# Expert stage of a three-block layer: 23 tiles of 256 sorted tokens of one expert in place of 40 of 128

## What is computed

```
x = x + cross_attention(norm(x), ctx)      # 16 heads, 257 context rows per sequence, 96 wide
x = x + time_mixing(norm(x))               # decayed running sums over the 32 positions
x = x + ffn(norm(x))
# ffn: expert = argmax(x @ Wr.T + br) of 8 experts; per token only that expert counts
h = relu(x @ W1[e].T + b1[e])              # 128 -> 512
y = h @ W2[e].T + b2[e]                    # 512 -> 128
```

## Time and profile before

| | |
|---|---|
| three runs | 1028.87, 1029.09 (median), 1031.62 us |
| span of the profiled execution, first to last instruction | 1027.0 us |
| busy: PE, DVE, POOL, ACT | 870.6, 831.1, 774.3, 684.0 us |
| scatter of the sorted rows, last landing | at 907.9 us |
| first product of the expert stage | at 913.2 us |
| start of the last indirect store | at 1019.8 us |

### The profile page before, as it was taken

One profiled execution on the slowest core, in us unless ns is written; L12 is line 12 of the kernel. 1 busy time (PEld: TensorE's weight loads), 2 busy tenths in 40 slices (PEclk: granted clock), 3 DMA queues, 4 the chain that ended last, 5 costly groups with the idle time before them and its releaser, 6 DMA issues.

```text
span 1027.0 us, 29818 instructions
## 1 busy us (share of the span) xinstructions
PE 870.6 (85%) x8554; PEld 720.6 (70%) x8554; DVE 831.1 (81%) x2343; ACT 684.0 (67%) x2029; POOL 774.3 (75%) x1237
## 2 busy tenths in 40 slices
PE   7989998999999999999999999999998461049895
PEld 7777786878787887878787887887776261036664
DVE  5899888989999989899999999998988657025563
ACT  3777776778777778778777777777775113037774
POOL 5788888898989898888889898989886503735554
PEclk9999999999999999999999999999999655559998
DMA  9111111111111111111111211111100840111120
GB/s 233 33 33 33 32 33 33 33 33 36 49 42 32 31 31 31 31 31 31 31 31 32 59 33 31 31 31 31 31 2 2 129 162 14 52 43 53 47 54 17
DMA packets 56836, 45.11 MB, mean 44 GB/s; under 512 B 8367, under 2 KB 54578, under 8 KB 56769
## 3 DMA queue, kind: packets, MB, share of 16 engines
q1 hardware_dynamic: 54464, 40.01, 15.9%
q0 software_dynamic: 2304, 4.25, 1.3%
HBM read 37.25 MB, written 7.52 MB: 44 GB/s over the span
## 4 chain that ended last, share of the span: by engine, by line
PE 36%; POOL 31%; issue 13%; DVE 12%; ACT 4%; DMA 1%; POOLq 1%; DVEq 1%; ACTq 0%; SPq 0%
POOL Pn L925 10%; PE bank L396 6%; PE bank L373 6%; PE bank L420 4%; POOL cT L916 4%; PE bank L1369 3%; PE bank L413 3%; PE bank L385 3%; POOL sorted_rows L1232 3%; POOL chi L906 2%; PE bank L1384 2%; DVE cs L839 2%; DVE nmax L783 2%; POOL clo L910 2%; DVE Tl L777 1%
## 5 line engine op out<-in xcount | busy, mean ns | idle before, releaser
L925 POOL TENSOR_TENSOR Pn<-Pe,rsum 128x1028 f32<-128x1028 f32 x128 | 243.1, 1899 | 74.4 <-DVE rsum L798 74.4
L713 ACT ACTIVATE Pe<-bank,nmax 128x257 f32<-128x257 f32 x512 | 240.5, 475 | 30.1 <-DVE nmax L783 29.5
L783 DVE TENSOR_REDUCE nmax<-bank 128x1 f32<-128x257 f32 x512 | 202.0, 415 | 35.3 <-PE bank L373 34.0
L373 PE MATMUL bank<-cT,qh 96*128 96x257 f16 x1024 | 184.8, 275 | 21.1 <-ACT Pe L713 19.6
L777 DVE TENSOR_TENSOR Tl<-bank,Th 128x512 f16<-128x512 f32 x256 | 173.8, 680 | 0.5 <-ACT Th L702 0.4
L702 ACT ACTIVATE Th<-bank 128x512 f16<-128x512 f32 x256 | 141.3, 595 | 48.5 <-PE bank L420 48.5
L420 PE MATMUL bank<-identf,Pn 128*128 128x128 f32 x1024 | 149.3, 274 | 0.0
L373 PE MATMUL bank<-cT,ql 96*128 96x257 f16 x512 | 139.2, 272 | 0.0
L420 PEld LDWEIGHTS bank<-identf,Pn 128*128 128x128 f32 x1024 | 115.1, 142 | 6.1
L373 PEld LDWEIGHTS bank<-cT,qh 96*128 96x128 f16 x1024 | 90.3, 97 | 38.3 <-issue 15.9
L713 ACT ACTIVATION_READ_ACCUMULATOR Pe<-bank,nmax 128x1 f32 x512 | 103.8, 203 | 0.0
(11 more groups left out here) (213 smaller groups left out, 2444.4 us busy)
## 6 DMA issues: line engine op xcount, KB each, us to landing
rawT<-in_dram SPq DMA_DIRECT2D x32, 385.5 KB, 3.9
raw<-in_dram SPq DMA_DIRECT2D x32, 384.0 KB, 4.4
sorted_rows<-fill SPq DMA_DIRECT2D x1, 2620.0 KB, 21.1
xs<-sorted_rows SPq DMA_DIRECT2D x40, 65.5 KB, 1.8
R<-in_dram SPq DMA_DIRECT2D x4, 512.0 KB, 5.9
Z<-last_rows SPq DMA_DIRECT2D x128, 2.2 KB
w1r<-in_dram SPq DMA_DIRECT2D x4, 512.0 KB, 13.7
w2fr<-in_dram SPq DMA_DIRECT2D x4, 512.0 KB, 14.2
```

Source lines behind the costliest of these rows:

```text
L373: last = nc.tensor.matmul(bank[SB[t]][:, 0:M], w[:, par, b, t * P:(t + 1) * P], cT[:, s4, c, 0:M], start=(k == 0), stop=(k == 2))
L713: nc.scalar.activation(Pe[:, n_par(j + 1), t, :], bank[SB[t]][:, 0:M], ACT.Exp, bias=nmax[:, n_par(j + 1), t:t + 1], accum_out=sums[:, n_p ...
L783: nc.vector.tensor_reduce(nmax[:, n_par(j + 1), t:t + 1], bank[SB[t]][:, 0:M], AX.X, ALU.max, negate=True).then_inc(s_nmax, 1)
L925: nc.gpsimd.tensor_tensor(Pn[:, par, :, :], Pe[:, par, :, :], rsum[:, par, :].unsqueeze(2).broadcast_to([P, QT, M]), ALU.mult)\
```

## The change

The sorted rows are laid out in tiles of TR = 256 rows. For 4096 tokens and eight experts that takes at most 4096/256 + 7 = 23 tiles, each of 256 rows of one expert (5888 rows in the buffer in place of 5120). Every buffer of a tile is twice as wide. By engine: the first layer's products have 256 columns, and each tile's hidden values take two banks (2 and 3, or 4 and 5), each reported when it is full, so `s_t["h"]` counts two for a tile. There are two transposes for a tile, both in bank 0. The second layer is done for both halves of 128 rows (m = 0, 1), in banks 6 and 7, and in another order of its products; these banks are the same for each tile, so PE waits for `out` of the tile just before. DVE norms a tile with two instructions. POOL stores a tile with two indirect transfers. SP's loads are written out. The packed experts have 3 integers in place of 5. The diff, cut to its core:

```diff
@@ -73,10 +73,13 @@
-    NT = G + E
+    SUB = 2
+    TR = SUB * P
+    NT = TOK // TR + E - 1
...
-    NK = NT // PK
+    NK = -(-NT // PK)
+    NL = NK * PK
@@ -88,7 +91,8 @@
-        bank = [top.enter_context(nc.psum_tensor(f"bank{i}", [P, 512], F32)) for i in range(8)]
+        psum = top.enter_context(nc.psum_tensor("bank", [P, 8, 512], F32))
+        bank = [psum[:, i, :] for i in range(8)]
@@ -304,8 +308,8 @@
@@ -318,37 +322,37 @@
...
-        ge = lsb("ge", [P, NT, E])
-        te = lsb("te", [P, NT])
-        tep = lsb("tep", [P, NT])
+        ge = lsb("ge", [P, NL, E])
+        te = lsb("te", [P, NL])
+        tep = lsb("tep", [P, NL])
...
-        xs = lsb("xs", [P, UN, RW])
-        xsn = lsb("xsn", [P, 2, C])
-        xsh = lsb("xsh", [P, 2, P], F16)
-        xsl = lsb("xsl", [P, 2, P], F16)
-        hr = lsb("hr", [P, 2, FC, P])
-        hh = lsb("hh", [P, UN, FC, P], F16)
-        hl = lsb("hl", [P, UN, FC, P], F16)
-        yb = lsb("yb", [P, UN, C + 1])
-        yout = lsb("yout", [P, UN, C])
-        idx = lsb("idx", [P, UN], U32)
+        xs = lsb("xs", [P, UN, SUB, RW])
+        xsn = lsb("xsn", [P, 2, SUB, C])
+        xsh = lsb("xsh", [P, 2, TR], F16)
+        xsl = lsb("xsl", [P, 2, TR], F16)
+        hr = lsb("hr", [P, 2, FC, TR])
+        hh = lsb("hh", [P, UN, FC, TR], F16)
+        hl = lsb("hl", [P, UN, FC, TR], F16)
+        yb = lsb("yb", [P, UN, SUB, C + 1])
+        yout = lsb("yout", [P, UN, SUB, C])
+        idx = lsb("idx", [P, UN, SUB], U32)
...
...
-        sorted_rows = nc.dram_tensor("sorted_rows", [NT * P, RW], F32, kind="Internal").ap()
+        sorted_rows = nc.dram_tensor("sorted_rows", [NT * TR, RW], F32, kind="Internal").ap()
@@ -358,6 +362,10 @@
+        def h_bank(v, f):
...
+            return bank[2 + SUB * v + f // SUB][:, (f % SUB) * TR:(f % SUB + 1) * TR]
@@ -1052,7 +1060,7 @@
-            for it in range(NT // UN + 2):
+            for it in range((NT + 2) // UN + 2):
@@ -1149,7 +1157,7 @@
-                         fill[:, :].unsqueeze(1).broadcast_to([P, NT, RW])).then_inc(s_fill, 16)
+                         fill[:, :].unsqueeze(1).broadcast_to([P, NT * SUB, RW])).then_inc(s_fill, 16)
             for h in range(4):
@@ -1157,18 +1165,14 @@
-            def load_tile(s, u):
+            for s in range(NT):
+                u = s % UN
...
-                sp.dma_start(xs[:, u, :], sorted_rows[bass.ds(P * s, P), :]).then_inc(s_xs[u], 16)
...
+                sp.dma_start(xs[:, u, :, :], sorted_rows[TR * s:TR * (s + 1), :].rearrange("(m p) c -> p m c", p=P))\
+                    .then_inc(s_xs[u], 16)
...
-                load_tile(u, u)
-            with sp.Fori(1, NT // UN) as i:
-                for u in range(UN):
-                    load_tile(UN * i + u, u)
-            for u in range(UN):
-                sp.wait_ge(s_store[u], 16 * (NT // UN))
+                sp.wait_ge(s_store[u], 16 * SUB * len(range(u, NT, UN)))
@@ -1209,9 +1213,9 @@
-            nc.gpsimd.iota(kk[:, :, :], pattern=[[0, E], [P, G]], base=0, channel_multiplier=0,
+            nc.gpsimd.iota(kk[:, :, :], pattern=[[0, E], [TR, TOK // TR]], base=0, channel_multiplier=0,
...
-            nc.gpsimd.iota(ti[:, :, :], pattern=[[1, NT], [0, E]], base=0, channel_multiplier=0,
+            nc.gpsimd.iota(ti[:, :, :], pattern=[[1, NL], [0, E]], base=0, channel_multiplier=0,
@@ -1230,7 +1234,7 @@
             for g in range(G):
...
-                                             R[:, g, :], None, bounds_check=NT * P - 1).then_inc(s_sorted, 16)
+                                             R[:, g, :], None, bounds_check=NT * TR - 1).then_inc(s_sorted, 16)
...
             def pool_tile(it, u, expert):
@@ -1241,14 +1245,15 @@
-                    nc.gpsimd.tensor_tensor(yb[:, w, :], xs[:, w, 0:C + 1],
-                                            b2b[:, bass.ds(e, 1), :].rearrange("p o c -> p (o c)"), ALU.add)\
+                    nc.gpsimd.tensor_tensor(yb[:, w, :, :], xs[:, w, :, 0:C + 1],
+                                            b2b[:, bass.ds(e, 1), :].broadcast_to([P, SUB, C + 1]), ALU.add)\
...
                 if exists(s - 3, NT):
...
-                    nc.gpsimd.indirect_dma_start(out_rows, bass.IndirectOffsetOnAxis(ap=idx[:, v:v + 1], axis=0),
-                                                 yout[:, v, :], None, bounds_check=TOK - 1, oob_is_err=False)\
-                        .then_inc(s_store[v], 16)
+                    for m in range(SUB):
+                        nc.gpsimd.indirect_dma_start(out_rows, bass.IndirectOffsetOnAxis(ap=idx[:, v, m:m + 1], axis=0),
+                                                     yout[:, v, m, :], None, bounds_check=TOK - 1, oob_is_err=False)\
+                            .then_inc(s_store[v], 16)
@@ -1286,16 +1291,16 @@
-                    wait(act, s_t["h"], s + 1)
...
                     for f in range(FC):
-                        last = nc.scalar.activation(hr[:, v, f, :], bank[2 + v][:, f * P:(f + 1) * P], ACT.Relu,
-                                                    bias=b1T[:, bass.ds(FC * e + f, 1)])
+                        if f % SUB == 0:
+                            wait(act, s_t["h"], SUB * s + f // SUB + 1)
+                        last = nc.scalar.activation(hr[:, v, f, :], h_bank(v, f), ACT.Relu, bias=b1T[:, bass.ds(FC * e + f, 1)])
...
                 if exists(s + 2, NT):
-                    wait(act, s_t["h"], s + 1)
+                    wait(act, s_t["h"], SUB * (s + 1))
...
-                    nc.scalar.activation(xsh[:, u % 2, :], bank[u % 2][:, 0:P], ACT.Copy).then_inc(s_t["xh"], 1)
+                    nc.scalar.activation(xsh[:, u % 2, :], bank[0][:, 0:TR], ACT.Copy).then_inc(s_t["xh"], 1)
                 if exists(s, NT):
@@ -1366,24 +1371,28 @@
                     for f in range(FC):
...
-                            last = nc.tensor.matmul(bank[2 + v][:, f * P:(f + 1) * P],
+                            last = nc.tensor.matmul(h_bank(v, f),
...
-                    last.then_inc(s_t["h"], 1)
+                        if f % SUB == SUB - 1:
+                            last.then_inc(s_t["h"], 1)
                 if exists(s + 2, NT):
...
-                    wait(pe, s_t["xl"], s + 1)
-                    nc.tensor.transpose(bank[v][:, 0:P], xsn[:, v, :], identf[:, :]).then_inc(s_t["xT"], 1)
+                    wait(pe, s_t["xl"], s + 2)
+                    for m in range(SUB):
+                        last = nc.tensor.transpose(bank[0][:, m * P:(m + 1) * P], xsn[:, v, m, :], identf[:, :])
+                    last.then_inc(s_t["xT"], 1)
                 if exists(s - 2, NT):
...
-                    wait(pe, s_t["out"], s - 3)
+                    wait(pe, s_t["out"], s - 2)
...
                     for f in range(FC):
-                        for k, (a, w) in enumerate(((hh, W2h), (hh, W2l), (hl, W2h))):
-                            last = nc.tensor.matmul(bank[4 + v][:, 0:C], a[:, (u - 2) % UN, f, :],
-                                                    w[:, bass.ds(e, 1), f * P:(f + 1) * P].rearrange("p o c -> p (o c)"),
-                                                    start=(f == 0 and k == 0), stop=(f == FC - 1 and k == 2))
+                        for k, (a, w) in enumerate(((hh, W2h), (hl, W2h), (hh, W2l))):
+                            for m in range(SUB):
+                                last = nc.tensor.matmul(bank[6 + m][:, 0:C], a[:, (u - 2) % UN, f, m * P:(m + 1) * P],
+                                                        w[:, bass.ds(e, 1), f * P:(f + 1) * P].rearrange("p o c -> p (o c)"),
+                                                        start=(f == 0 and k == 0), stop=(f == FC - 1 and k == 2))
@@ -1441,14 +1450,14 @@
-            r.link(nc.vector.tensor_tensor(gt[:, :, :], run[:, G - 1, :].unsqueeze(2).broadcast_to([P, E, G]), kk[:, :, :],
+            r.link(nc.vector.tensor_tensor(gt[:, :, :], run[:, G - 1, :].unsqueeze(2).broadcast_to([P, E, TOK // TR]), kk[:, :, :],
...
-            r.mark(nc.vector.tensor_tensor(ge[:, :, :], ti[:, :, :], ends[:, :].unsqueeze(1).broadcast_to([P, NT, E]),
+            r.mark(nc.vector.tensor_tensor(ge[:, :, :], ti[:, :, :], ends[:, :].unsqueeze(1).broadcast_to([P, NL, E]),
...
-            r.link(nc.vector.scalar_tensor_tensor(before[:, :, :], offs[:, :].unsqueeze(1).broadcast_to([P, G, E]), float(P),
+            r.link(nc.vector.scalar_tensor_tensor(before[:, :, :], offs[:, :].unsqueeze(1).broadcast_to([P, G, E]), float(TR),
@@ -1459,7 +1468,7 @@
-            digit = lambda k: tep[:, k:NT:PK]
+            digit = lambda k: tep[:, k:NL:PK]
@@ -1476,28 +1485,30 @@
                 if exists(s + 2, NT):
...
-                    wait(dve, s_t["h"], s + 1)
+                    wait(dve, s_t["h"], SUB * (s + 1))
...
-                    nc.vector.tensor_tensor(xsl[:, v, :], bank[v][:, 0:P], xsh[:, v, :], ALU.subtract)\
+                    nc.vector.tensor_tensor(xsl[:, v, :], bank[0][:, 0:TR], xsh[:, v, :], ALU.subtract)\
...
```

(35 more changed lines are left out.)

## The result

The changed kernel takes 1015.36 us (median of 4 runs, 1015.09 to 1021.06), the kernel before 1029.49 us beside it (4 runs, 1028.87 to 1031.62). The ratio of the runs, as recorded with its 95% interval, is 0.9884 (0.9858 to 0.9911): 1.2% faster. The two medians alone give 0.986, inside that interval. The profiled execution took 1015.09 us with a span of 1013.0. The stage, from its first first-layer product to the end of the span, took 1027.0 - 913.21 = 113.8 us before and takes 1013.0 - 912.96 = 100.0 now.

What follows compares the result with a forecast made beforehand. PE and a second, equally tight loop bound the old step (2.56 us); afterwards PE's wait for yout would. Start, 3.7 us steps and drain end the span at 1014.8, 12.2 less; against the 1029.1 median, 1017 us, range 1008 to 1025.

Steps and rivals of the forecast that it cites:

- the likeliest case: Whole kernel: added wait sets the step at 3.7 us; 1017 us, range 1013 to 1020, chance 0.48.
- The step: Expert stage: two-step loop of 7.3 us through yout and PE's second layer; 3.65 us a tile, 3.7 with packed-expert reads.
- Second layer: PE: 24 products of 128 columns take 1.33 us, since register instructions for a product are halved.
- Hand-over and transposes: PE: 0.23 us from second layer to next first layer, 0.4 for two transposes; PE's own step 3.3 us.
- if POOL runs without a wait, it is the bound: Sign against the forecast: POOL running without a wait would mean POOL, not the loop, sets the step.
- the slower rival: PE falls back to half clock in the added waits: step 4.95 us, 24 us more, 1041 us; chance 0.07.
- my sign (below 0.95 after 925): Sign against the forecast: PE's granted clock falls below 0.95 after 925 us.
- Start, drain, tail: Stage ends: first product 914.0, clock rise within 2 us of 921.65, last store 1007.6, span end 7.2 us later.
- Cover of the longer fill: SP's queue: 15% longer buffer fill costs nothing behind the 41 us scatter; without that cover some 3 us.
- The shorter loop: Expert stage: DVE's queue or ACT's first half is quicker; POOL or PE sets step 3.4, 1011 us; chance 0.2.
- the stretched one: Second layer keeps its old pitch (1.96 us) or POOL's stores stretch: step 4.0, 1023 us; chance 0.18.
- the rival of no gain: Longer loop eats the fewer steps without the clock: step 4.2 to 4.7, 1026 to 1032 us; chance 0.07.

Runs made afterwards that it cites:

- the two faster kernels: Changed kernel with yout before hl on DVE, plus half the stores dropped (997.59 us) or yb taken off POOL and bias added by PE (1004.07 us).
- half the stores: Changed kernel with one of each tile's two output transfers dropped, half the output rows unwritten: 1014.39 us, ratio 0.9883.

## Why the prediction was right

1017 was said and 1015.4 measured, within the likeliest case's own 1013 to 1020. By the steps:

- **The step.** 3.7 said, 3.675 measured (19 steps in 69.8 us, where I had 929.8 - 925.8 + 66.6 = 70.6). The mechanism is the one named: moving `yout` forward takes 0.47 off, cutting POOL's work takes nothing off, and 0.21 us put into the loop costs 0.108 a step. In the stretch shown, the last first-layer product starts at 930.65; `xsh` comes 1.38 later (1.34 said), `hh` 1.64 (1.68), `hl` 2.89 (2.84), `yout` 4.09 (4.04), PE's second layer at 935.34 after 4.69 (4.55). Two steps on, tile 7's first layer has its last product at 936.68 + 1.20 = 937.88, 7.23 after the start of this count (7.3). PE's second layer waits for `yout` in nearly every step, as I had said. The long and short distances in turn I had not said: the loop spans two steps, so there are two of them, through the even and the odd tiles. A round takes 7.1 to 7.8 us, and nothing spaces the two evenly.
- **First layer.** 1.20 us for 1.22 said. But wide products are not why PE is quick: split in two they take 1.28.
- **Second layer.** 24 products took 933.51 + 0.11 - 932.29, less one pitch, some 1.28 us (1.33 said), 0.056 each. That halving the register instructions would bring the pitch back has come true; that they are its cause is argued, not shown. The rule of 81 ns (the Trainium skill, TensorE: Matmul & The Clock Gate, Back-to-back issue gap) would have made it 1.9 us; no row of the changed kernel shows it, so that rival fell.
- **Hand-over and transposes.** I had 0.23 us from the last product to the next first layer and 0.4 for two transposes; measured are 0.11 and 0.22. PE's own step is so 1.20 + 0.11 + 0.22 + 1.23 + 0.11 = 2.87 us and not 3.3. Nothing hung on it here, since the loop is longer. It would have decided in the two faster kernels: their steps of 3.01 and 3.09 lie below the 3.3 that I took for PE's limit.
- **POOL.** 2 x 1.19 for the transfers from 925 to 995, 0.71 for `yb` and 0.48 between them are 3.57 us (3.6 said). It is busy for 51.0 of the 60 us from 925 to 985, 85%, but for 78% of the stretch from 920 to 1000. My sign "if POOL runs without a wait, it is the bound" was wrong, and the rows show how it came to run without one. There is no backlog: POOL starts on 15 of the tiles 1 to 18 between 0.44 and 0.63 us after their `yout` has ended (932.10, then `yb` at 932.55). Where it has to wait, it starts about 0.25 after it (924.92, then 925.17, and nearly always with half the stores). In ten of these steps the second transfer of the tile before is held up by `hl` until 0.84 us after `hl`, and `yout` ends 0.40 after `hl`. So the stretching of the transfer fills the time in which POOL would have waited, and from `yb` to `yb` it takes (991.07 - 928.40)/17 = 3.69 us, the loop's own step. The experiment was needed to tell.
- **The clock.** It stayed up, 0.99 from 920 to 1000 us, with PE idle for up to 1.3 us in every second step: the slower rival had its waits and not its fall. It did fall once, in the drain, behind an idle time of 2.6 us, so the letter of my sign (below 0.95 after 925) was met there:

```profile
997.93 0.27 PE L1393 MATMUL bank<-W2h,hh 128*128 x2 [2.60 <-DVE hl L1503]
...
998.82 0.34 PE L1393 MATMUL bank<-W2l,hh 128*128 x2
998.96 0.42 PE L1393 MATMUL bank<-W2h,hh 128*128 x2
```

  Most of the last second layer then ran with pairs 0.21 apart instead of 0.11, granted clock 0.50 from 999 to 1002. The last two second layers took 1.45 and 2.10 us from the first to the last pair where the others take 1.22, 1.1 us more. The prediction had no such term; it is more than the 0.8 us by which the drain misses below.
- **Start, drain, tail.** The first product came at 912.96 (914.0 said). The clock rose between 916 and 918 us, where I kept the old 921.65 within 2 us, so the last product of tile 3's first layer started at 922.34 + 1.20 = 923.5 and not 925.8: -2.3, of which -1.0 is the first product. The steps gave -0.8, the drain from e(22) = 993.4 to the last store 12.0 in place of 11.2, +0.8, and the span ended 1013.0 - 1005.35 = 7.65 after that store, not 7.2, +0.45. Together -1.8: 1013.0 for 1014.8. That the sum came so near owes something to luck, since -3.1 and +1.3 cancel in part. The drain is the term whose path was wrong: I had POOL behind with three pairs of stores in a row. In fact `yout` of tile 20 ended 4.38 us after e(22) (4.45 said), but then two of the three pairs waited for their own `yout` (they start at 998.54 and 1004.08, 0.8 us after it), and the pace was that of PE's second layers of tiles 21 and 22, each waiting for the `yout` before. What brought the clock's rise forward is not shown. The window of the rise:

```profile
916.00:918.00 2.00, 1.92 (x13) 1.26 (x11) 0.95 (x4) 2.00 (x5) 0.00 (x0) 0.76 0.00 0
```

- **Cover of the longer fill.** The fill of the sorted buffer now lands after 25.5 us and the loads of tiles after 2.2; the first product was no later for it:

```profile
sorted_rows<-fill SPq DMA_DIRECT2D x1, 3013.0 KB, 25.5
xs<-sorted_rows SPq DMA_DIRECT2D x23, 131.0 KB, 2.2
```

- **The other rivals.** The shorter loop (3.4) and the stretched one (4.0) both missed the step by 0.3, and the rival of no gain needed 4.2. Transfers did stretch, to 1.19 on the mean, but not beyond what the loop left POOL.
- **What of the 13.8 us is what.** 40 steps of 2.56 are 102.4 us, 23 of 3.675 are 84.5: 17.9 less. 17.9 - 13.8 = 4.1 are given back at the ends of the stage, and the traces say where. From the first product to the start of the last tile's first layer it was 99.0 us before (tile 39 at 1012.24) and is 79.2 now (tile 22 at 992.16), 19.8 less. From there to the end of the span it was 14.8 and is 20.8. So 6.1 us are lost behind the last tile, and nothing at the start.

## What to carry to other kernels

When tiles are doubled and a buffer loses its double for it, write down the new loop through all engines, queue position by queue position: here the arithmetic of that loop gave the step to 1%. Then ask what stands in front of the reader of that buffer on its own engine; moving one small instruction ahead of a long one was worth 0.47 us a step and no memory. An engine that never waits need not be the bound: only taking work off it tells, and the same cut can be worth nothing before a wait is shortened and 0.2 us a step after it. And a wait that has left the list of waits need not be gone: compare the start of the instruction with the end of what it waits for.

## What the hardware showed that I had not expected

A row of a transfer on POOL's timeline is the instruction that starts it, not the way of its data. Of the 38 that start between 926 and 995 us, 26 take 0.97 to 1.06 us and 12 take 1.10 to 1.95, and DVE decides which. The timelines of POOL and DVE in the changed kernel:

```profile
930.61 1.93 POOL L1254 DMA_INDIRECT out_dram<-yout,idx  x1 [0.30 <-issue]
...
941.15 1.93 POOL L1254 DMA_INDIRECT out_dram<-yout,idx  x1 [0.16 <-issue]
...
991.99 0.99 POOL L1254 DMA_INDIRECT out_dram<-yout,idx  x1 [0.16 <-issue]
```

```profile
940.99 1.21 DVE L1503 TENSOR_TENSOR hl<-hr,hh 128x1024 f16<-128x1024 f32 x1
...
992.02 1.22 DVE L1503 TENSOR_TENSOR hl<-hr,hh 128x1024 f16<-128x1024 f32 x1 [1.41 <-ACT hh L1307]
```

The twelve are just those that start while an `hl` is running, and each ends 0.83 to 0.88 us after it: `hl` of 930.47 ended at 931.70 and the transfer at 932.54, `hl` of 940.99 ended at 942.20 and the transfer at 943.08. A transfer that has started when `hl` begins is hardly touched: the one of 991.99 started 0.03 before `hl` and took 0.99, and six that started 0.10 to 0.12 before one took 1.05 or 1.06 and ended before `hl` did. So the sentence ahead of the run with `hl` in four, that whatever overlaps `hl` ends 0.84 after it, holds only for transfers that start inside it. As the rows have it, something at the start of the instruction can't be done while `hl` runs, and once past it the rest goes on. With `hl` in four pieces the longest takes 1.15.

The Trainium skill (SBUF — State Buffer, SBUF: two separate sides) says that DVE and GpSimd share a pair of ports, which one instruction holds for its whole length while the other stands still. A DVE instruction with two SBUF inputs does so only against a GpSimd instruction that reads SBUF; that GpSimd can't write the descriptors of its transfers meanwhile is said of DVE's modes with two ports. The traces agree that the length of DVE's instruction is what counts. `hl` has two SBUF inputs, and the transfer takes its row numbers from SBUF, so the rule may be the first one; no run separates them. The Trainium skill (same section) has a stalled transfer end some 115 ns after DVE's instruction; here it is 0.84 us, near the full length of a transfer.

It works the other way too. The groups of lines from 905 to 1015 us in the kernel with `yout` first, where DVE and POOL meet more often:

```profile
L1497 DVE TENSOR_SCALAR xsn<-xs 128x128 f32<-128x128 f32 x46 | 21.9, 517 | 38.3 <-DMA xs<-sorted_rows 38.3
```

The mean of the same instruction is 393 ns in the changed kernel. Here it is `yb` that it meets: the pair takes 0.59 us at 929.86 in the changed kernel, beside a transfer alone, and 1.01 at 940.06, with `yb` from 940.17 to 940.99. Neither engine's busy time is its own: a part of each is waiting for the other, and the profile counts it as work.
